# A graph layer streamed in 64 items: feature blocks loaded later, one half row earlier, three evacuations moved

## The reference

```python
def _gcn_layer(x, adj, W, b):
    d_inv_sqrt = (jnp.sum(adj, axis=1) + 1e-09) ** (-0.5)
    msg = d_inv_sqrt[:, None] * adj * d_inv_sqrt[None, :] @ x
    return jax.nn.relu(msg @ W + b)
H_f = _gcn_layer(feature_x, adj, W_f, b_f)
H_s = _gcn_layer(spatial_x, adj, W_s, b_s)
attn = jax.nn.sigmoid(jnp.concatenate([H_f, H_s], axis=1) @ W_att + b_att)
y = attn * H_f + (1.0 - attn) * H_s
out = _layernorm(x + y)          # eps 1e-5, along the 128 columns
```

## Time and profile before

| | |
|---|---|
| time, median of 3 runs | 420.37 us (420.26 to 420.81) |
| the profiled execution | 420.79 us, of which the span of the profile is 419.0 us |
| PE busy | 375.0 us (90%) |
| DVE, ACT, POOL busy | 289.3, 286.1, 146.3 us |
| transfers | 132.84 MB, mean 317 GB/s |
| PE waits that the profile shows, over 1 us | until 13.7 us, then at 29, 69, 77, 84, 119, 210, 388 and 403 us |

### The profile page before, as it was taken

The page is one execution under the profiler, slowest core; times in us unless marked ns, Lnnn a source line. Parts: engine busy times, 40 slices in busy tenths (PEclk is TensorE's granted clock), DMA queues, the critical chain, the costliest instruction groups (busy, mean ns, idle before and its releaser), DMA issues. The chain is left out here.

```text
span 419.0 us, 5128 instructions
## 1 busy us (share of the span) xinstructions
PE 375.0 (90%) x1680; PEld 309.4 (74%) x1680; DVE 289.3 (69%) x401; ACT 286.1 (68%) x346; POOL 146.3 (35%) x199
## 2 busy tenths in 40 slices
PE   0689998699969999999899999999999999998940
PEld 0567887588858887888678888888888888887830
DVE  2569983496366957597655959388757886977554
ACT  3768588877888749787888687674433676576453
POOL 1203001021000881059200899251000556643664
PEclk9999999999989999999989999999999999999965
DMA  8999999999999999999999999897555444350001
GB/s 312 389 425 421 417 422 421 421 421 420 422 420 422 415 342 418 422 419 422 423 418 422 413 415 375 320 380 268 199 190 187 192 128 165 111 175 27 25 26 51
DMA packets 25530, 132.84 MB, mean 317 GB/s; under 512 B 2848, under 2 KB 7712, under 8 KB 11296
## 3 DMA queue, kind: packets, MB, share of 16 engines
q1 hardware_dynamic: 25504, 132.53, 79.1%
HBM read 130.42 MB, written 2.10 MB: 316 GB/s over the span
## 5 line engine op out<-in xcount | busy, mean ns | idle before, releaser
L356 PE MATMUL sums<-Ah,Yh 128*128 128x512 f32 x512 | 203.4, 397 | 25.5 <-DVE Yl L432 18.3
L421 DVE TENSOR_TENSOR Al<-raw,Ah 128x2048 fp32r<-128x2048 f32 (+1 forms) x70 | 152.3, 2179 | 90.7 <-ACT Ah L552 89.5
L358 PE MATMUL sums<-Al,Yh 128*128 128x512 f32 x512 | 201.4, 393 | 0.0
L357 PE MATMUL sums<-Ah,Yl 128*128 128x512 f32 x512 | 201.3, 393 | 0.0
L552 ACT ACTIVATE Ah<-raw 128x2048 fp32r<-128x2048 f32 (+1 forms) x70 | 123.4, 1767 | 54.2 <-DMA raw<-in_At 30.2
L356 PEld LDWEIGHTS sums<-Ah,Yh 128*128 128x128 f32 x512 | 97.6, 191 | 49.0 <-DVE Yl L432 19.5
L565 ACT ACTIVATE nat<-nat 128x2048 f32<-128x2048 f32 x53 | 101.6, 1917 | 19.2 <-DMA nat<-in_adj 17.9
L358 PEld LDWEIGHTS sums<-Al,Yh 128*128 128x128 f32 x512 | 97.3, 190 | 20.7
L357 PEld LDWEIGHTS sums<-Ah,Yl 128*128 128x128 f32 x512 | 97.7, 191 | 19.8
L444 DVE TENSOR_TENSOR acc<-sums,acc 128x512 f32<-128x512 f32 x112 | 71.5, 682 | 6.3 <-PE sums L358 6.3
L657 POOL TENSOR_SCALAR dg<-rs 128x1 f32<-128x1 f32 x22 | 14.1, 640 | 150.6 <-ACT nat L565 150.3
(11 more groups left out here) (43 smaller groups left out, 112.1 us busy)
## 6 DMA issues: line engine op xcount, KB each, us to landing
raw<-in_At SPq DMA_DIRECT2D x63, 1024.0 KB, 10.0
nat<-in_adj SPq DMA_DIRECT2D x56, 1024.0 KB, 11.6
xs<-in_xs SPq DMA_DIRECT2D x7, 512.0 KB, 11.2
out<-xs SPq DMA_DIRECT2D x32, 64.0 KB, 1.7
raw<-in_At SPq DMA_DIRECT2D x4, 256.0 KB, 9.8
xs<-in_xs SPq DMA_DIRECT2D x1, 384.0 KB, 9.2
xs<-in_xs SPq DMA_DIRECT2D x1, 128.0 KB, 2.4
watt<-in_W_att SPq DMA_DIRECT2D x1, 128.0 KB, 10.3
```

The costliest lines, as they stand in the source:

```text
L356: pe.matmul(to, Yh[:, t % YRING, hs], high, start=first, stop=False)
L357: pe.matmul(to, Yl[:, t % YRING, hs], high, start=False, stop=False)
L358: mm = pe.matmul(to, Yh[:, t % YRING, hs], low, start=False, stop=last)
L421: dve.tensor_tensor(Al[:, k % SPLITS, a * IB:b * IB], raw[:, k % RAWS, a * IB:b * IB], Ah[:, k % SPLITS, a * IB:b * IB], ALU.subtract).the ...
```

## The change

Three edits. Feature blocks 2 to 7 are issued after items 12, 20, 28, 36, 39 and 43. Half row 4 (tile 2) is issued and summed at item 3, where half rows 4 and 5 stood both at item 4. On DVE the evacuation of the run that ended at item k - 2 comes ahead of `low(k)` also for k = 17, 25 and 33. Nothing is added or removed: the instructions and bytes are the same.

```diff
-    for k, r in [(0, 0), (1, 1), (4, 2), (5, 3), (8, 4), (9, 5), (10, 6), (11, 7)]:
+    for k, r in [(0, 0), (1, 1), (5, 3), (8, 4), (9, 5), (10, 6), (11, 7)]:
         parts[k] = [2 * r, 2 * r + 1]
+    parts[3], parts[4] = [4], [5]
...
     SHARED = [0, 1, 3]
+    X_AFTER = {6: 1, 12: 2, 20: 3, 28: 4, 36: 5, 39: 6, 43: 7}
+    EVACUATE_FIRST = [k for k in range(K) if k < 2 * G or k in (17, 25, 33)]
...
                 load_item(k)
-                if k == 6:
-                    load_x(1)
-                if k % G == G - 1 and k // G + 2 < G:
-                    load_x(k // G + 2)
+                if k in X_AFTER:
+                    load_x(X_AFTER[k])
...
                 ended = [e for e in evac_order if end_item[e] == k - 2]
-                evacuate_new(ended if k < 2 * G else ended[:1] if len(ended) == GT else [])
+                evacuate_new(ended if k in EVACUATE_FIRST else ended[:1] if len(ended) == GT else [])
```

## The result

| | before | after |
|---|---|---|
| time, median of 4 runs each | 420.44 us (420.26 to 420.81) | 427.75 us (427.32 to 428.22) |
| the profiled execution | 420.79 us | 427.8 us |
| its span | 419.0 us | 426.0 us |

What follows compares the result with a forecast made beforehand. The prediction took the kernel as bound by PE and the stretches where PE is not fed. Item 35 starting later (+4.2 us) plus slow clock (+2.0) gave +6.2 us: 426.6 us on the median's footing, range 424.3 to 429.2.

Steps and rivals of the forecast that it cites:

- The step that decides: At tile 20's `Yh`, ACT waits for block 5 until 221.4 us; PE begins item 35 4.2 us later, at 228.3.
- The slow clock behind it: After PE's idle time of about 10 us before item 35, slow matmuls cost 2.0 us, between 1.5 and 2.7.
- PE decides at item 40, not the feed: At item 40 the feed comes 4.6 us later and PE 6.2 us later, so PE decides by 1.4 us.
- POOL's sums of item 38: Item 38's blocks, issued at 228.2 us on an empty queue, land at about 236 us, 4.6 us later than before.
- rival D: Feed of items 38 to 40 takes over, item 38's blocks 2 us later or POOL slower: 428.6 to 430 us; chance 0.15.
- The total: Whole kernel: +4.2 us at item 35 plus 2.0 us of slow clock, +6.2 us, 426.6 us on the median's footing.
- The early gains: Later feature blocks and earlier evacuations bring PE to item 34 up to 6.4 us earlier, at about 212.5 us.
- Item 9 was to lose its whole wait: With block 2 behind item 12, items 8 to 12 land 1.25 us earlier and item 9's 1.12 us wait goes.
- a growing wait: PE's wait at item 24 may grow, as PE comes earlier than `Yl` of tile 14 lets DVE go on; no size.
- Rival A: Wait at tile 20's `Yh` does not bind, PE keeps up to 6.4 us from item 34: 414.4 us; chance 0.04.

Runs made afterwards that it cites:

- part 2: Kernel before with only half row 4 loaded and summed at item 3 and half row 5 alone at item 4: 420.48 us, ratio 1.0002.
- the last kernel: Evacuations ahead, last half rows later, group 7 sums on DVE behind low part, block 5 and tile 20 at item 36, plus tile 23's degree earlier on POOL: 423.21 us.

## Why the prediction was right, and where it was off

**The step that decides: right.** It said that ACT would stand at tile 20's `Yh` until 221.5 us; it stood until 221.84. Sum of the half row 221.9 (222.25), high part of item 35 at 223.8 (224.14), low part at 225.9 (226.17), PE at 228.3 (228.61). Each step is 0.3 us late, all of it from the landing of block 5. PE's idle time was to be about 10 us and was 9.72. That one transfer causes it is shown by moving it alone (same loss) and by putting it back, or its user behind it (loss gone).

**The slow clock behind it: right, a little under-sized.** 2.0 us were taken between bounds of 1.5 and 2.7; it was 2.29 us.

**PE decides at item 40, not the feed: right.** 257.5 us forecast, 258.10 measured, with no idle time before items 36 to 40. One term in it was off, and another made up for it. POOL's sums of item 38 started at 237.83 us, not 236. The working had item 38's blocks on an empty queue, but the queue had filled again by then, with half row 45, item 37's blocks and half row 46 ahead, and they took 9.3 us to land where one megabyte on the empty queue took 5.2. That is nearly the 2 us that rival D asked for. But DVE's low part, which had fallen into the fourth of these additions before, starts only at the end of them now (243.46 us), and the four took 6.15 us where they took 7.48 before. The low part of item 40 came 5.4 us later than before, ready at 256.5 us with PE at 258.10:

```profile
253.78 2.75 DVE L422 TENSOR_TENSOR Al<-raw,Ah 128x2048 fp32r<-128x2048 f32 x1 [0.79 <-ACT Ah L553]
```

So PE decided by 1.6 us, much as forecast (1.4), but partly by luck: the shorter sums were not in the working.

**The total.** +6.2 us forecast, +7.3 on the medians and +7.0 in the profiled executions. Of the difference of 0.8 us in the latter, 0.3 is the landing, 0.3 the clock, and 0.26 comes between items 43 and 45 (5.68 and 5.57 us for two items that took 5.53 and 5.44 before); for that last part, which is within what two traces differ by, no cause was found.

**The early gains: right in direction.** Item 34 at 213.29 us against 212.5 forecast; but about 2 us of the lead of 5.4 there is the slow clock behind item 32 in the one trace of the kernel before, which another trace of that order does not have (part 2). Item 9 was to lose its whole wait of 1.12 us and kept 0.58, so 0.8 of the 1.2 us came in this trace; in the three other kernels with these blocks later it starts at 67.66 to 67.92 us with no wait over 0.5 us, as forecast. At item 24 the forecast allowed for a growing wait; it came, and leaves item 25 only 2.5 us early.

**Rival A was mis-priced.** It was given 414.4 us, on the ground that the 6.4 us at item 34 would stay if the wait did not bind. The wait was taken away in two ways and cut to 4.29 us in a third, and the times were 421.15, 421.22 and 421.17 us. The gain reaches item 34 and goes no further: the transfer stream and an evacuation behind the low part take a part at item 36, the chain through POOL's sums and tile 23's degree takes the rest at item 40. The prediction had noted that the feed of item 40 had no slack, and used it only for the case of a late PE. The same row says what an early PE gets, and A should have been priced from it at about 420 us. The change at its best is thus no gain: these three kernels are 0.2 to 0.4% slower than before, where the evacuations alone and the half row alone are at 1.0000 and 1.0002. That leaves moving blocks 2 to 4, 6 and 7, alone or with the rest, and why it costs 0.2% was not isolated; in the kernel with block 5 back, item 36 starts at 227.49 us with a halved clock behind it, against 226.84 without in the evacuations-only kernel.

**What stays open.** What decides whether the clock falls behind a wait of 2 to 3 us, and with it 1.6 us in some executions. And what block 5 one item later still would do was not tried. By the order of the waits it would never end: SP would issue block 5 behind half row 45, half row 45 only after half row 42 is summed, and that sum stands on ACT behind tile 20, which waits for block 5.

## What to carry to other kernels

Before a load is issued later, find the instruction that waits for it and read what stands behind that instruction on its engine: everything in that queue waits too. The price is nothing while a later place without slack hides it, and then nearly the whole delay (nothing for block 5 behind item 35, 6.6 us behind item 36); moving the user along with the load removed it here. A gain at one item is worth only what the next place without slack lets through; price the good case from that place as carefully as the bad one. When work is spread to a second engine, look at what the two do at the same moment, since it may make both longer.

## What the runs showed of the hardware that I had not expected

- In ten of the traces PE waits 2.33 to 2.79 us at item 35 or 36, all with a saturated transfer stream. The granted clock fell behind seven of these waits (7.13 to 7.17 us for the item behind) and stayed at 1.00 behind three, of 2.38, 2.40 and 2.78 us (5.53, 5.56 and 5.84 us). So the length of a wait of this size did not tell whether a slow restart follows. In the kernel before a wait of 1.86 us was followed by a granted clock of 0.66 over 3 us (part 2). After 9.72 us of idle time it was halved.
- Four additions of 128 x 512 float32 on DVE, all operands in SBUF, took 3.08 us by themselves. They took 3.98, 4.89 and 6.89 us where one, two and all four of them met an addition of the same kind on POOL: about 0.9 us more for each. It goes both ways. In the changed kernel one POOL addition overlaps a low part on DVE by 0.94 us, and that low part takes 3.10 us instead of the 2.29 of the earlier trace rows. The next POOL addition starts during that low part and takes 3.16 us instead of 1.29:

```profile
246.90 1.29 POOL L695 TENSOR_TENSOR S<-S,raw 128x512 f32<-128x512 f32 x1
...
248.34 3.16 POOL L695 TENSOR_TENSOR S<-S,raw 128x512 f32<-128x512 f32 x1
```

```profile
247.25 3.10 DVE L422 TENSOR_TENSOR Al<-raw,Ah 128x2048 fp32r<-128x2048 f32 x1
```

The Trainium skill, SBUF — State Buffer (SBUF: two separate sides), says that a DVE operation with two SBUF inputs and a POOL operation that reads SBUF exclude each other, and that whichever comes second waits until the first instruction is done. The trace agrees for this pair: 0.94 us of overlap, 0.81 us longer. In the last kernel, with the rows taken one by one, the two engines take turns: POOL's additions start at 242.02, 243.73 and 245.43 us, DVE's at 242.53, 244.24 and 245.94. A pair takes 1.70 us. By themselves the two take 1.29 and 0.68 us, 1.97 one after the other, so the rule gives most of the size here, but not all of it.

- A load of one megabyte took 5.2 us from issue to landing on an empty queue, against a median of 10.0 us for the items' blocks before and 12.5 us for item 36's. The fourth load after the queue had run dry took 9.3 us again.
